# Causal attention with the triangle added in VectorE's maximum and zeros written by GpSimd, in place of mask products on TensorE

## What is computed

```python
def attention(x, wq, wk, wv, wo, bo):
    b, t, _ = x.shape
    q = (x @ wq).reshape(b, t, HEADS, HEAD_DIM)
    k = (x @ wk).reshape(b, t, HEADS, HEAD_DIM)
    v = (x @ wv).reshape(b, t, HEADS, HEAD_DIM)
    scores = jnp.einsum('bqhd,bkhd->bhqk', q, k)
    mask = jnp.arange(t)[:, None] < jnp.arange(t)[None, :]
    scores = jnp.where(mask, -jnp.inf, scores)
    attn = jax.nn.softmax(scores / np.sqrt(HEAD_DIM), axis=-1)
    ctx = jnp.einsum('bhqk,bkhd->bqhd', attn, v).reshape(b, t, EMB)
    return ctx @ wo + bo
```

## Time and profile before

| what | value |
|---|---|
| time, median of 3 runs | 4730.88 us (4717.94 to 4744.70) |
| span of the profiled execution | 4737.0 us |
| busy share of the span: PE, DVE, ACT, POOL | 88%, 64%, 52%, 24% |
| first causal attention: first max item to last back | 3556.3 to 3889.0 us |
| second causal attention | 4190.6 to 4520.2 us |

### The profile page before, as it was taken

One profiled execution on the slowest core, in us unless ns is written; L12 is line 12 of the kernel. 1 busy time (PEld: TensorE's weight loads), 2 busy tenths in 40 slices (PEclk: granted clock), 3 DMA queues, 4 the chain that ended last, 5 costly groups with the idle time before them and its releaser, 6 DMA issues.

```text
span 4737.0 us, 62689 instructions
## 1 busy us (share of the span) xinstructions
PE 4164.9 (88%) x23278; PEld 1984.9 (42%) x23280; DVE 3026.0 (64%) x6690; ACT 2453.6 (52%) x4189; POOL 1126.0 (24%) x1579
## 2 busy tenths in 40 slices
PE   8888879999898889999886778999988989889999
PEld 5222335655522236555552235555552334333343
DVE  4888467777588857776337974666666653466622
ACT  3588634555358764555346543445534663236642
POOL 1100113333200013333023651111130014420034
PEclk9799988999879998999888998999987999969999
DMA  1100102111100011110000000000011000000000
GB/s 50 28 15 15 46 0 75 37 31 38 41 21 18 11 57 36 31 40 19 5 11 0 0 8 8 9 16 16 9 38 24 21 7 0 29 22 23 14 0 9
DMA packets 48017, 104.07 MB, mean 22 GB/s; under 512 B 15064, under 2 KB 15064, under 8 KB 46432
## 3 DMA queue, kind: packets, MB, share of 16 engines
q1 hardware_dynamic: 46560, 98.49, 7.6%
q10 hardware_dynamic: 1152, 1.57, 0.1%
HBM read 40.24 MB, written 1.05 MB: 9 GB/s over the span
## 4 chain that ended last, share of the span: by engine, by line
PE 61%; DVE 24%; ACT 8%; POOL 3%; issue 2%; DMA 1%; ACTq 1%; SPq 0%; POOLq 0%; DVEq 0%
PE PS L447 29%; PE PS L1123 8%; PE PS L1071 7%; DVE SM L1197 6%; PE PS L1103 3%; PE PS L2644 3%; DVE AR L2448 2%; ACT AR L454 2%; DVE AR L451 2%; PE PS L1757 1%; PE PS L1747 1%; PE PS L474 1%; PE PS L1076 1%; ACT AR L1171 1%; ACT PS L2392 1%
## 5 line engine op out<-in xcount | busy, mean ns | idle before, releaser
L1197 DVE TENSOR_REDUCE SM<-PS 128x1 f32<-128x512 f32 (+3 forms) x1792 | 1029.2, 627 | 241.0 <-PE PS L1071 158.8
L447 PE MATMUL PS<-AR,WS 128*128 128x512 f32 (+1 forms) x2112 | 1057.8, 640 | 77.3 <-DVE AR L451 31.0
L1171 ACT ACTIVATE AR<-PS 128x1024 f32<-128x1024 f32 (+3 forms) x896 | 826.4, 934 | 342.9 <-PE PS L1106 173.7
L454 ACT ACTIVATE AR<-PS 128x512 f32<-128x512 f32 (+4 forms) x728 | 440.3, 615 | 520.0 <-PE PS L447 389.3
L1071 PE MATMUL PS<-AR 51*128 51x512 bf16 (+3 forms) x1792 | 527.9, 391 | 143.3 <-DVE SM L1197 99.3
L447 PEld LDWEIGHTS PS<-AR,WS 128*128 128x128 f32 (+1 forms) x2112 | 402.5, 202 | 541.3 <-issue 409.8
L1123 PE MATMUL PS<-AR 128*32 128x512 f32 (+3 forms) x3584 | 452.5, 578 | 1.3 <-ACT AR L1171 0.9
L1828 ACT ACTIVATE AR<-PS,SM 128x128 f32<-128x128 f32 x512 | 229.9, 453 | 424.0 <-DVE SM L1891 418.3
L1071 PEld LDWEIGHTS PS<-AR 51*128 51x128 bf16 x1792 | 130.0, 94 | 662.0 <-DVE SM L1197 477.4
L1103 PE MATMUL PS<-AR 51*128 51x512 bf16 (+3 forms) x1792 | 387.0, 367 | 11.8 <-ACT AR L1171 11.0
L1230 POOL CAST MBT<-SM 128x8 bf16<-128x8 f32 x128 | 28.2, 220 | 1265.5 <-DVE SM L1201 1065.9
(11 more groups left out here) (323 smaller groups left out, 7119.5 us busy)
## 6 DMA issues: line engine op xcount, KB each, us to landing
TP<-RAW SPq DMA_DIRECT2D x512, 64.0 KB, 2.0
AR<-AR SPq DMA_DIRECT2D x720, 32.0 KB
WS<-wall SPq DMA_DIRECT2D x4, 3654.5 KB, 11.0
WS<-wall SPq DMA_DIRECT2D x8, 902.5 KB, 4.6
WS<-wall SPq DMA_DIRECT2D x2, 3334.5 KB, 10.3
WS<-wall SPq DMA_DIRECT2D x1, 2384.0 KB, 9.0
WS<-wall SPq DMA_DIRECT2D x1, 1543.5 KB, 6.1
AR<-AR ACTq DMA_DIRECT2D x48, 32.0 KB
```

The lines of the kernel that those rows point to most:

```text
L447: t = e.matmul(o, l, r, start=(n == 0), stop=(n == len(pairs) - 1))
L454: return e.activation(o, i, ACT.Copy, scale=1.0)
L1171: e.activation(pv[:, :, off:512], sv[:, :, off:512], ACT.Exp, scale=scale).then_inc(*F.at_exp.up((s, u, p2)))
L1197: e.tensor_reduce(mh[:, at, k0 // 512:k0 // 512 + 1], bank(ring(n + g), m), AX.X, ALU.max, negate=True).then_inc(*F.at_max.up((s, k, i, rr ...
```

## The change

Four edits, all of them for the causal attentions but for a sign:

- TensorE's mask products (lines 1076 and 1106) are gone. Each score product now ends its own bank and reports by itself, where a masked item reported only after the mask product.
- For a max item on the diagonal VectorE's `tensor_reduce` becomes a `tensor_tensor_reduce`: it adds a slice of a new bf16 constant `MASKED` (384 columns of zeros and then the triangle) to the scores, takes the maximum, and writes the sums to a scratch slot of f32 in SBUF that nobody reads. The item waits for the third masked maximum before it (for the slot), which the same engine has long finished.
- After the exponential of a diagonal front GpSimd writes zeros over the part above the diagonal, 128 columns for each of the two heads in one `affine_select`, and the back waits for the second of the unit's two selects. GpSimd now walks through the same list of items as the others: splits of maxima and selects stand in its queue in the order of the list.
- Maxima are kept with their own sign, the pad rows hold -1 in place of 1, and the joining of halves is a maximum. This touches the other two attentions too, with the same instructions in number and size. The constants loaded at the start are 512 bf16 columns wider (1320 to 1832).

```diff
-    pad[0:3] = 1
+    pad[0:3] = -1
...
+            ("MASKED", np.concatenate([np.zeros((128, 384)), np.where(k <= i, 0, NEG)], 1))], pad
...
-        H16 = ctx.enter_context(nc.sbuf_tensor("H16", [128, 1320], BF16))
+        H16 = ctx.enter_context(nc.sbuf_tensor("H16", [128, 1832], BF16))
...
-                    diag = causal and k0 + m == wide
...
-                        t = e.matmul(bank(p, m), l, r, start=True, stop=not diag)
-                        if not diag:
-                            t.then_inc(*F.at_scores_max.up((s, k, i, rr, k0, g)))
-                    if diag:
-                        for g in range(2):
-                            e.matmul(bank(ring(n + g))[:, m - 128:m], H["I"], H["LOWQ"], start=False, stop=True).then_inc(
-                                *F.at_scores_max.up((s, k, i, rr, k0, g)))
+                        e.matmul(bank(p, m), l, r, start=True, stop=True).then_inc(*F.at_scores_max.up((s, k, i, rr, k0, g)))
...
-                    diag = causal and 128 * kti >= 512 * qc
                     for g in range(2):
...
-                        t = e.matmul(sv[:, g, off:512], l, r, start=True, stop=not diag)
-                    if diag:
-                        for g in range(2):
-                            t = e.matmul(sv[:, g, off:off + 128], H["I"], H["LOWK"], start=False, stop=True)
+                        t = e.matmul(sv[:, g, off:512], l, r, start=True, stop=True)
...
                     w.wait_ge(*F.at_exp.on((s, u, 1)))
+                    if causal and 128 * kti >= 512 * qc:
+                        w.wait_ge(*F.at_masked.on((s, u, 1)))
...
-                        e.tensor_reduce(mh[:, at, k0 // 512:k0 // 512 + 1], bank(ring(n + g), m), AX.X, ALU.max,
-                                        negate=True).then_inc(*F.at_max.up((s, k, i, rr, k0, g)))
+                        top = mh[:, at, k0 // 512:k0 // 512 + 1]
+                        if causal and k0 + m == wide:
+                            w.wait_ge(*F.split_low.on((s, 7)))
+                            if len(masked) >= 3:
+                                w.wait_ge(*F.at_max.on(masked[-3]))
+                            masked.append((s, k, i, rr, k0, g))
+                            e.tensor_tensor_reduce(out=slot(5 + len(masked) % 3, m), in0=bank(ring(n + g), m), in1=H["MASKED"][:, 512 - m:512], scale=1.0, scalar=-3.0e38,
+                                                   op0=ALU.add, op1=ALU.max, accum_out=top).then_inc(*F.at_max.up((s, k, i, rr, k0, g)))
+                        else:
+                            e.tensor_reduce(top, bank(ring(n + g), m), AX.X, ALU.max).then_inc(*F.at_max.up((s, k, i, rr, k0, g)))
...
+                if kind == "front" and causal:
+                    u, p2 = args
+                    k, qc, kti, nk = units[u]
+                    off = 128 * kti - 512 * qc
+                    if off >= 0:
+                        own = PR[(2 * u + p2) % 4].rearrange("p (j t) -> p j t", j=2)[:, :, off:off + 128]
+                        w.wait_ge(*F.at_exp.on((s, u, p2)))
+                        e.affine_select(out=own, in_=own, pattern=[[0, 2], [1, 128]], compare_op=ALU.is_ge, fill=0.0, base=0,
+                                        channel_multiplier=-1).then_inc(*F.at_masked.up((s, u, p2)))
```

More of the change, by code:

```diff
@@ L56, in half_arrays @@
     pad = np.zeros((128, 4096), np.float32)
-    pad[0:3] = 1
+    pad[0:3] = -1
     return [("I", np.eye(128)), ("LOWQ", np.where(k <= i, 0, NEG)), ("LOWK", np.where(i <= k, 0, NEG)),
             ("BAND", np.where(band, 0, NEG)), ("BAND0", np.where(band & (own | (i >= 64)), 0, NEG)), ("EXP8", three(np.kron(np.eye(16), np.ones((1, 8))))),
-            ("EXP64", three(np.kron(np.eye(8), np.ones((1, 64))))), ("J8", three(np.eye(8))), ("J32", three(np.eye(32)))], pad
+            ("EXP64", three(np.kron(np.eye(8), np.ones((1, 64))))), ("J8", three(np.eye(8))), ("J32", three(np.eye(32))),
+            ("MASKED", np.concatenate([np.zeros((128, 384)), np.where(k <= i, 0, NEG)], 1))], pad
 def rope_tables():
@@ L1185, in attention_dve @@
         def attention_dve(e, w, s, causal, add):
+            masked = []
             for kind, n, *args in order[causal]:
@@ new lines, in attention_pool @@
+            units = units_of[causal]
+            for kind, n, *args in order[causal]:
+                if kind == "max":
+                    k, i, rr, k0 = args
+                    wide = 128 * (i + 1) if causal else 1024
+                    if not (i % 2 and rr and k0 + 512 >= wide):
+                        continue
+                    pair = 4 * k + i // 2
+                    mb, mf = MB[pair % 2], MF[pair % 3]
+                    m8 = mf[:, 16:24] if wide > 512 else mf[:, 0:16].rearrange("p (n h) -> p n h", h=2)[:, :, 0]
+                    m8, r8 = m8.rearrange("p (n g) -> p n g", g=2), mf[:, 24:32].rearrange("p (n g) -> p n g", g=2)
+                    if pair >= 2:
+                        w.wait_ge(*F.at_max_turned.on((s,) + pairs_of_max[pair - 2]))
+                    if wide > 512:
+                        w.wait_ge(*F.at_max_all.on((s, k, i)))
+                    else:
+                        w.wait_ge(*F.at_max.on((s, k, i, 1, 0, 1)))
+                    e.tensor_copy(mb[:, :, :, 0], m8).then_inc(*F.pool_step.up())
+                    w.wait_ge(*F.pool_step.newest())
+                    e.tensor_tensor(r8, m8, mb[:, :, :, 0], ALU.subtract).then_inc(*F.pool_step.up())
+                    w.wait_ge(*F.pool_step.newest())
+                    e.tensor_copy(mb[:, :, :, 1], r8).then_inc(*F.pool_step.up())
+                    w.wait_ge(*F.pool_step.newest())
+                    e.tensor_tensor(mb[:, :, :, 2], r8, mb[:, :, :, 1], ALU.subtract).then_inc(*F.at_max_parts.up((s, k, i)))
+                if kind == "front" and causal:
[7 more added lines that the diff above has]
+                                        channel_multiplier=-1).then_inc(*F.at_masked.up((s, u, p2)))
```

22 lines of the change are left out of this document (2 added, 20 removed).

## The result

The changed kernel takes **4649.9 us** (median of 4 runs, 4637.3 to 4657.2) against 4732.2 for the kernel before (4 runs, 4717.9 to 4744.7). The ratio is 0.9826, with a 95% interval of 0.9805 to 0.9846: faster by 1.7%, where 4648 us was forecast. The profiled execution took 4657.2 us; its span is 81.6 us shorter than the span of before.

What follows compares the result with a forecast made beforehand. TensorE was taken to fill the causal attentions' middles. Per attention −42 − 2 + 2 = −42, twice −84, plus 1 for constants: −83, span 4654, median 4648 us, eight-in-ten range 4595 to 4735.

Steps and rivals of the forecast that it cites:

- the middle: Stretch of each causal attention where max items, fronts and backs mix, now 276.9 us in the first: forecast 230 to 240.
- TensorE's release: Middle of a causal attention: removing mask products frees 64 us of TensorE's time, 0.39 us per item.
- VectorE's steps: Middle: VectorE's 1.13 us per item plus 0.285 gives 1.41 against 1.663, a gain of 42 us per attention.
- The price of 0.33 us for a masked item: Middle: TensorE time a masked max item loses with its mask products, taken from 0.61 against 0.23 us, at most 0.38.
- VectorE's second instruction: Masked maxima: writing the result adds 0.15 us each, range 0 to 0.28, or 0.20 per item.
- Turn-taking: Middle: TensorE and VectorE alternating over three banks adds 0.285 us per item over VectorE's steps, from the unmasked attention.
- The first stretch: Max items alone at the attention's start, 31.7 us: TensorE's saving set against VectorE's twice 0.15 us, counted as 0.
- The last stretch: Fronts and backs alone at the attention's end, 26.1 us: exponentials start sooner, −2 us.
- GpSimd: Middle: selects of 0.64 us each, splits sometimes delaying them, +2 us per attention; backs wait no more than a few us.
- VectorE busy over 80%: Sign of a right forecast: VectorE busy for over 80% of the middle stretch.
- Rival 1: VectorE becomes the bound: slower masked maxima give 4831 us; break-even at 0.34 us per masked maximum; chance 0.13.
- Rival 3: Middle: granted clock falls to 0.70, item 1.62 against 1.663 us, only the ends gain, 4727 us; chance 0.15.

Runs made afterwards that it cites:

- experiment 3: Changed kernel with a second 128-column product per masked max product, beside its own product or behind both products of the item: 4658.2 and 4669.7 us.
- experiment 5: Changed kernel without GpSimd's select and the back's wait for it, the upper triangle staying in the exponentials: 4655.4 us, ratio 0.9836.
- experiment 7: Changed kernel with every GpSimd select issued twice, one behind the other: 4693.1 us, ratio 0.9911.
- either half alone: Changed kernel with only its new maxima (fronts as before), 4688.8 us, or only its new fronts with selects (maxima as before), 4733.7 us.
- the front part: Changed kernel's fronts with GpSimd selects, but maxima as in the kernel before (TensorE mask product, plain maximum): 4733.7 us, ratio 1.0008.
- the four orders: Changed kernel with causal max items dealt unevenly, leaning to wide fronts (4687.3, 4704.6 us) or to narrow ones (4704.5, 4697.4 us).

## Why the prediction was right, and where its terms were off

The direction and the mechanism were right: mask products leave TensorE's queue, and VectorE's new pass costs what the plain maximum cost. The total (4648 forecast, 4649.9 measured) and the length of the middle (230 to 240 forecast, 228.9 and 236.4 measured in the cut of the earlier trace rows) came close too, but that they fit so closely is in part luck: several of the terms were off and made up for one another. The profiled attentions gained 91.6 us together where 84 were forecast, and a rest that was 10 us longer in this execution, with 1 forecast, hides it.

- **TensorE's release.** The 64 us of the prediction are what its sum lost in the first attention (254.1 to 190.1), 51 in the second. The 42 us per attention by VectorE's steps stand against 48 and 37 in the cut of the earlier trace rows (276.9 to 228.9, 273.6 to 236.4). The price of 0.33 us for a masked item, taken from starts, is near the 0.31 that the medians of experiment 3 give. But *why* a pair costs that was not asked, beyond naming the change of weights. Experiment 3 shows two products of the same width to be worth some 6 of 27 us when they run beside the other head's. By the Trainium skill's 81 ns per product (TensorE: Matmul & The Clock Gate, "Back-to-back issue gap") the sum was 36 us in place of 64; the two mask products themselves start 0.07 us apart, and what that count leaves out is the waits before and behind the pair. To keep the rows' price was right.
- **VectorE's second instruction**, 0.15 us forecast (range 0 to 0.28), is 0.02. That is 0.17 us less per item, 28 us per attention.
- **Turn-taking**, 0.285 us per item carried over from the attention without a mask, is too small: 328 maxima in 228.9 us are 1.396 us per item, VectorE's steps are 0.93 + 1.33 × 0.02 = 0.96, so 0.44 lies between. The unmasked attention has no narrow items and no selects. The two errors nearly cancel (1.41 forecast, 1.40 measured, 1.45 in the second attention). The sum was right and its parts were not.
- **The first stretch**, counted as 0, gained 8 us each time, 16 together. TensorE and VectorE take turns there, as the prediction itself read in the earlier trace rows; then a pair taken from TensorE's turn shortens the round. I set it against 0.15 us of VectorE that did not come. **The last stretch**, −2, is 0.
- **GpSimd**: 0.41 us per select for 0.64, and the +2 us not visible. The backs' waits, 11.5 us in this middle, are more than the "few us" that I named, and cost nothing that experiment 5 finds. With the two selects of experiment 7, 0.84 us, the 2 us became 16 per attention.
- **VectorE busy over 80%** was wrong (76%), for the same reason as the second instruction.
- **Rival 1** did not come, at 0.02 us per masked maximum; its break-even was nearer (about 0.20) than I had it (0.34). **Rival 3**, the clock, did not come to the changed kernel (0.94 and 0.89), but to either half alone: the front part's 12 us per attention were halved in the profiled execution, as the clock went from 0.92 to 0.88, and gone in the median. Its sum was also not carried through: 1.62 against 1.663 us per item leaves 0.04, 7 us per attention, so 4713 in place of 4727. The Trainium skill's warning (TensorE: Matmul & The Clock Gate, "HAM oscillation — how this bites in real kernels") that gaps between bursts bring the clock down goes the same way as the lower clocks of the halves and of the four orders. No run here shows the gaps to come first, and the changed kernel, with fewer products in its middle than either half (1495), kept its clock.

**Open:** why the clock stays up with both halves and not with one, and whether the clock causes the length or follows it; and how much of the middle's gain is the barrier of the 128-row products, beyond the estimate of experiment 3.

## What to carry to other kernels

When small products with few rows run in pairs, one from row 0 and one from row 64, look at the starts around whatever full-height product stands between them: here it waited until the products before it were nearly done and held up those behind it, and by the estimate above that wait, not the product, was most of the cost. When two engines take turns, an engine at three quarters busy can pass on four fifths of what is added to it, as VectorE did here, so price additions in full and look for the break-even by doubling the suspected instruction. And before adding up parts tested alone, compare their granted clocks: a part worth 29 us at equal clock read as 0 here.

## What the runs showed that I had not expected

- A VectorE add-and-maximum with its result costs what the plain maximum costs: 686 ns at 512 columns, its result read in 83 ns beside the next pass, 0.02 us more per step at the most where masked ones follow each other. Two that depend on each other step by 0.59 us in place of 0.48 at 384 columns.
- A GpSimd select of 128x256 f32 takes 406 ns, less than the copy of that size, 447 ns.
- Between 0.73 and 0.94 the middles' granted clock followed the mix of work, down when VectorE was given more, down when max items were dealt unevenly, and not up when TensorE was given 214 more products (0.88 and 0.91 against 0.94 and 0.89).
